# Second-layer expert weights split into half-precision parts inside each job: a perceiver layer on one Trainium2 core

## The reference

```python
def _moe_forward(x, gate_w, gate_b, w1, b1, w2, b2, ln_g, ln_b):
    logits = (x @ gate_w + gate_b) / TEMP
    topk_vals, topk_idx = jax.lax.top_k(logits, TOP_K)
    ...
    h = jnp.einsum('bsd,edf->bsef', x, w1) + b1
    h = jax.nn.gelu(h, approximate=False)
    expert_out = jnp.einsum('bsef,efd->bsed', h, w2) + b2
    out = jnp.einsum('bse,bsed->bsd', gate_probs, expert_out)
    ...
```

## Time and profile before

| | |
|---|---|
| median of three runs | 1473.92 us (1472.44 to 1474.47) |
| the profiled execution's own time | 1473.72 us |
| its span, first to last instruction | 1472.1 us |
| mean granted TensorE clock | 0.972 |
| TensorE busy over the span | 1371.9 us |
| VectorE, ScalarE busy | 780.4 us, 586.5 us |
| groups repeat every | 92.9 us |
| jobs repeat every | 26.4 us |

### The profile page before, as it was taken

How to read it: one execution, slowest core, us unless ns; L and a number is a source line. 1 busy time by engine, 2 the same in 40 slices (tenths; PEclk the granted TensorE clock), 3 DMA queues, 4 the chain that set the end, 5 groups by cost and what they waited for, 6 DMA issues and landing times.

```text
span 1472.1 us, 24339 instructions
## 1 busy us (share of the span) xinstructions
PE 1371.9 (93%) x7888; PEld 870.2 (59%) x7889; DVE 780.4 (53%) x1871; ACT 586.5 (40%) x1082; POOL 152.4 (10%) x200
## 2 busy tenths in 40 slices
PE   6879999999999999999985699999999999999997
PEld 5658677686776876768764344444444444444442
DVE  5665876878778777777665442222222222232225
ACT  3565665756757567465670211212112121121100
POOL 1001012020120200202003100000000000000005
PEclk9999999999999999999996799999999999999997
DMA  9693142341323413224028807523325166100005
GB/s 364 265 351 144 52 156 91 115 160 50 141 95 112 173 50 126 110 97 190 29 114 328 307 17 278 206 93 148 144 104 195 35 265 248 44 21 21 14 15 171
DMA packets 53566, 207.48 MB, mean 141 GB/s; under 512 B 4902, under 2 KB 5012, under 8 KB 47388
## 3 DMA queue, kind: packets, MB, share of 16 engines
q1 hardware_dynamic: 40320, 123.14, 22.8%
q0 software_dynamic: 13184, 83.89, 14.9%
q10 hardware_dynamic: 28, 0.01, 0.0%
HBM read 144.11 MB, written 62.91 MB: 141 GB/s over the span
## 4 chain that ended last, share of the span: by engine, by line
PE 82%; DVE 7%; ACT 4%; issue 4%; DMA 1%; POOL 1%; SPq 0%; DVEq 0%; ACTq 0%
PE bank L623 21%; PE bank L1458 8%; PE bank L1416 7%; PE bank L605 6%; PE bank L606 5%; PE bank L607 5%; PE bank L1379 4%; PE bank L1484 4%; PE bank L1400 3%; PE bank L615 3%; PE bank L1506 2%; PE bank L1425 2%; PE bank L1440 2%; ACT moe_w L951 2%; PE bank L1459 1%
## 5 line engine op out<-in xcount | busy, mean ns | idle before, releaser
L623 PE MATMUL bank<-moe_w,arena 128*128 x736 | 330.9, 592 | 0.0
L491 DVE SCALAR_TENSOR_TENSOR arena<-bank,now_scales,arena 128x512 f32<-128x512 f32 x92 | 69.1, 751 | 346.1 <-PE bank L607 346.1
L623 PEld LDWEIGHTS bank<-moe_w,arena 128*128 128x128 f32 x736 | 132.7, 190 | 132.5 <-issue 132.5
L1416 PE MATMUL bank<-moe_w 128*128 128x257 f32 x768 | 189.9, 385 | 6.5 <-DVE moe_w L883 6.5
L428 ACT ACTIVATE arena<-arena 128x512 f32<-128x512 f32 x92 | 58.3, 633 | 337.8 <-DVE arena L491 337.8
L1416 PEld LDWEIGHTS bank<-moe_w 128*128 128x128 f32 x768 | 138.2, 192 | 25.7 <-DVE moe_w L883 5.8
L605 PE MATMUL bank<-moe_w,arena 128*128 x368 | 140.6, 382 | 2.4 <-DVE arena L504 2.4
L606 PE MATMUL bank<-moe_w,arena 128*128 x368 | 140.4, 382 | 0.0
L607 PE MATMUL bank<-moe_w,arena 128*128 x368 | 140.2, 381 | 0.0
L1458 PE MATMUL bank<-moe_w 128*128 128x512 f16 x384 | 114.4, 379 | 10.0 <-ACT moe_w L940 7.0
L926 ACT ACTIVATE moe_w<-bank,cols,ugain 128x512 f32<-128x512 f32 x96 | 74.6, 777 | 61.6 <-PE bank L1459 60.8
(11 more groups left out here) (230 smaller groups left out, 2129.1 us busy)
## 6 DMA issues: line engine op xcount, KB each, us to landing
moe_w<-w_halves POOLq DMA_DIRECT2D x8, 4096.0 KB, 13.3
moe_w<-in_L_ffn_w_dram POOLq DMA_DIRECT2D x8, 4096.0 KB, 24.4
w_halves<-moe_w SPq DMA_DIRECT2D x48, 512.0 KB, 2.7
xs_rows<-blocks SPq DMA_DIRECT2D x8, 2048.0 KB, 14.8
moe_w<-in_L_ffn_w_dram SPq DMA_DIRECT2D x16, 1024.0 KB, 6.4
arena<-in_ctx_dram SPq DMA_DIRECT2D x32, 384.0 KB
arena<-in_L_ffn_w_dram SPq DMA_DIRECT2D x8, 1024.0 KB, 4.8
blocks<-in_L_ffn_w_dram SPq DMA_DIRECT2D x8, 1024.0 KB, 4.8
```

Of the source, the lines that this page charges most:

```text
L491: nc.vector.scalar_tensor_tensor(out=h_sb[:, fb % 2, :], in0=bank[fb % 2][:, :], scalar=now_scales[:, KD:KD + 1], in1=b1_rows[:, bass.ds(s ...
L623: last = nc.tensor.matmul(Y[:, :], hT_sb[:, fb % 2, c, :], moe_flat[:, bass.ds((e % 2) * 16384 + 8192 + (4 * fb + c) * DIM, DIM)], start=( ...
L1416: last = nc.tensor.matmul(bank[h][:, 0:KEYS], qkT[:, c, b, h * P:(h + 1) * P], cnT[:, b % 2, c, :], start=(c == 0), stop=(c == KC - 1))
```

## The change

The second layer is computed like the first, with three half-precision products instead of a full-precision one. The weights `w2` stay in full precision in memory and in `moe_w`; in each job they are turned into halves, one block's rows (128 x 2048) at a time, in two sets of buffers used in turn (`v_high`, `v_low`, in pieces of 1024 columns): `v_hi` on ScalarE, `v_lo` on VectorE, for block fb once `mm2` of two blocks before is done. The transposed hidden rows are split as well: `h_hi` on ScalarE out of PSUM, `h_lo` on VectorE in place of `hT_copy`. Scales for both are needed: in the first stage `row_sums2` (ScalarE) sums the magnitudes of every w2 row, from loads added to SP (`raw2_load`), and `most_of` and `scales_of` grow. ScalarE's loop in the expert stage becomes a `job` of its own; it holds no load of the activation table any more, only one ahead of it. The second half of the additions to `x_all` is moved from behind job 0 to behind job 1, and `diags` from behind job 1 to behind the last `y_copy`, since v_high and v_low take their space. The diff, cut:

```diff
+        v_high = [[y[:, :], yT[:, :, :].rearrange("p c t -> p (c t)")], [wosT[:, 2, :], wosT[:, 3, :]]]
+        v_low = [[kqT[:, :, :].rearrange("p c t -> p (c t)"), v_sb[:, :]],
+                 [arena[:, 7680:8192], blocks[:, :, :].rearrange("p h t -> p (h t)")[:, 1536:2048]]]
...
+            def h_hi(j, fb):
+                act.wait_ge(hT_full, FB * j + fb + 1)
+                if fb >= 2 or not isinstance(j, int) or j > 0:
+                    act.wait_ge(mm2_done, 1 + FB * j + fb - 1)
+                nc.scalar.activation(hT_high[:, fb % 2, :, :].rearrange("p c t -> p (c t)"), bank[2 + fb % 2][:, :], ACT.Identity,
+                                     scale=now_h[:, 0:1]).then_inc(hT_high_done, 1)
+
+            def v_hi(j, fb, slot):
+                if fb >= 2 or not isinstance(j, int) or j > 0:
+                    act.wait_ge(mm2_done, 1 + FB * j + fb - 1)
+                for i in range(2):
+                    nc.scalar.activation(v_high[fb % 2][i], moe_flat[:, bass.ds(slot * 16384 + 8192 + fb * 2048 + i * 1024, 1024)],
+                                         ACT.Identity, scale=now_v[:, 0:1]).then_inc(v_high_done, 1)
+
+            def job(j, first, last):
+                slot = act.value_load(job_e[0:1, bass.ds(j, 1)], min_val=0, max_val=EXPERTS - 1) % 2
+                gelu(j, 0)
+                if not first:
+                    h_hi(j - 1, 3)
+                act.wait_ge(now_h_ok, j + 1)
+                v_hi(j, 0, slot)
+                gelu(j, 1)
+                h_hi(j, 0)
+                v_hi(j, 1, slot)
+                gelu(j, 2)
+                h_hi(j, 1)
+                v_hi(j, 2, slot)
+                if not last:
+                    x_hi(j + 1)
+                gelu(j, 3)
+                h_hi(j, 2)
+                v_hi(j, 3, slot)
...
+            def h_scales_now(j, e):
+
+                if not isinstance(j, int) or j > 0:
+                    dve.wait_ge(hT_out, FB * j)
+                    dve.wait_ge(v_low_done, 2 * FB * j)
+                nc.vector.tensor_copy(now_v[:, :], job_scales[:, bass.ds(e, 1), KD + 1])
+                nc.vector.tensor_copy(now_h[:, :], job_scales[:, bass.ds(e, 1), KD + 2]).then_inc(now_h_ok, 1)
...
-            def hT_copy(j, fb):
...
+            def h_lo(j, fb):
+                dve.wait_ge(hT_high_done, FB * j + fb + 1)
...
+            def v_lo(j, fb, slot):
+                for i in range(2):
+                    dve.wait_ge(v_high_done, 2 * (FB * j + fb) + i + 1)
+                    nc.vector.scalar_tensor_tensor(out=v_low[fb % 2][i], in0=moe_flat[:, bass.ds(slot * 16384 + 8192 + fb * 2048 + i * 1024, 1024)],
+                                                   scalar=now_v[:, 0:1], in1=v_high[fb % 2][i],
+                                                   op0=ALU.mult, op1=ALU.subtract).then_inc(v_low_done, 1)
...
                 bias(j, 0, slot)
                 if not first:
-                    hT_copy(j - 1, 3)
+                    h_lo(j - 1, 3)
+                h_scales_now(j, e)
+                v_lo(j, 0, slot)
                 bias(j, 1, slot)
-                hT_copy(j, 0)
+                h_lo(j, 0)
                 if not first:
                     y_copy(j - 1)
+                y_scale_now(j, e)
+                v_lo(j, 1, slot)
                 bias(j, 2, slot)
-                hT_copy(j, 1)
+                h_lo(j, 1)
+                v_lo(j, 2, slot)
                 bias(j, 3, slot)
                 if not last:
                     dve.wait_ge(h_biased, FB * (j + 1))
                     scales_now(j + 1)
-                hT_copy(j, 2)
-                if not last:
                     x_lo(j + 1)
+                h_lo(j, 2)
+                v_lo(j, 3, slot)
...
+                pe.wait_ge(v_low_done, 2 * (FB * j + fb + 1))
                 for c in range(4):
...
+                    nc.tensor.matmul(Y[:, :], hT_low[:, fb % 2, c, :], high, start=(fb == 0 and c == 0), stop=False)
+                    nc.tensor.matmul(Y[:, :], hT_high[:, fb % 2, c, :], high, start=False, stop=False)
+                    last = nc.tensor.matmul(Y[:, :], hT_high[:, fb % 2, c, :], low, start=False, stop=(fb == 3 and c == 3))
...
+                if later:
+                    sp.wait_ge(sum2_done, KD * (g - 1) + 3)
+                    raw2_load(g - 1, 3, raw2)
+                    sp.wait_ge(sum2_done, KD * g)
+                    raw_load(g, 0)
...
+                sp.wait_ge(m_full, M_FILLS * g + O_AT + 2)
+                raw2_load(g, 0, raw2)
+                raw2_load(g, 1, raw2)
+                if not nxt:
+                    raw2_load(g, 2, raw2_last)
                 halves_store(g, 0)
-                halves_store(g, 1)
                 if nxt:
                     sp.wait_ge(halves_out[0], 32 * (g + 1))
-                    raw_load(g + 1, 0)
+                    raw2_load(g, 2, raw2)
+                halves_store(g, 1)
...
+            def row_sums2(g, k, of):
+
+                act.wait_ge(raw2_in[k], 16 * (g + 1))
+                if k == 0:
+                    at_least(act, sums2_kept, g)
+                nc.scalar.activation(of[k].bitcast(F16)[:, 0:FF], of[k], ACT.Abs, bias=tiny[:, 0:1], scale=W_SUM,
+                                     accum_out=row_sum2[:, k:k + 1]).then_inc(sum2_done, 1)
```

More of the change, by code:

```diff
@@ L42 @@
 X_MAX = 2.0 ** 10
+H_ROWS = 512.0
 GB = P // TOK
@@ L428, in gelu @@
                 nc.scalar.activation(h_sb[:, fb % 2, :], h_sb[:, fb % 2, :], ACT.Gelu).then_inc(h_act, 1)
-            x_hi(0)
[L431 to L437, removed]
+            def h_hi(j, fb):
[28 more added lines that the diff above has]
+                v_hi(j, 3, slot)
+            x_hi(0)
+            job(0, True, False)
+            with act.Fori(1, JOBS - 1) as j:
+                job(j, False, False)
+            job(JOBS - 1, False, True)
+            h_hi(JOBS - 1, 3)
         def moe_dve(dve):
@@ L543, in moe_dve, with x_and_beta @@
             x_lo(0)
+            def x_and_beta(first, n):
+                for t in range(first, first + n):
+                    last = nc.vector.tensor_tensor(x_all[:, t, :], x_all[:, t, :], lnrow[:, 1, :], ALU.add)
+                return last
             job(0, True)
             dve.wait_ge(rows_in, 48)
-            for t in range(GROUPS):
-                last = nc.vector.tensor_tensor(x_all[:, t, :], x_all[:, t, :], lnrow[:, 1, :], ALU.add)
-            last.then_inc(xb_done, 1)
+            x_and_beta(0, GROUPS // 2)
             job(1, False)
+            x_and_beta(GROUPS // 2, GROUPS // 2).then_inc(xb_done, 1)
+            with dve.Fori(2, JOBS - 1) as j:
+                job(j, False)
+            job(JOBS - 1, False, True)
+            h_lo(JOBS - 1, 3)
+            y_copy(JOBS - 1)
             for t in range(GROUPS):
@@ L621, in mm2 @@
                     pe.wait_ge(ys_out, j)
+                pe.wait_ge(v_low_done, 2 * (FB * j + fb + 1))
                 for c in range(4):
-                    last = nc.tensor.matmul(Y[:, :], hT_sb[:, fb % 2, c, :],
-                                            moe_flat[:, bass.ds((e % 2) * 16384 + 8192 + (4 * fb + c) * DIM, DIM)],
-                                            start=(fb == 0 and c == 0), stop=(fb == 3 and c == 3))
+                    high, low = [part[fb % 2][c // 2][:, (c % 2) * DIM:(c % 2 + 1) * DIM] for part in (v_high, v_low)]
+                    nc.tensor.matmul(Y[:, :], hT_low[:, fb % 2, c, :], high, start=(fb == 0 and c == 0), stop=False)
+                    nc.tensor.matmul(Y[:, :], hT_high[:, fb % 2, c, :], high, start=False, stop=False)
+                    last = nc.tensor.matmul(Y[:, :], hT_high[:, fb % 2, c, :], low, start=False, stop=(fb == 3 and c == 3))
                 last.then_inc(mm2_done, 1)
@@ L1019, in body @@
                     w_hi(g, 3)
+                    row_sums2(g, 0, raw2)
+                    row_sums2(g, 1, raw2)
+                if do_a and not nxt:
+                    row_sums2(g, 2, raw2_last)
+                    row_sums2(g, 3, raw2_last)
+                    act.wait_ge(b1_in, 16)
+                    nc.scalar.activation(b1_raw, b1_raw, ACT.Abs, bias=tiny[0:EXPERTS, 0:1], scale=W_SUM,
+                                         accum_out=b1_sum[:, :]).then_inc(b1_summed, 1)
             act.wait_ge(consts, 7)
@@ L1185, in body @@
                     cn_apply(0, 1)
+                if do_b and do_a:
+                    dve.wait_ge(sum2_done, KD * (g - 1) + 2)
                 for i in range(QK_PAIRS):
```

123 lines of the change are left out of this document (85 added, 38 removed).

## The result

The change took 1516.67 us (median of four runs, 1515.59 to 1518.34), the kernel before 1474.2 us beside it: a ratio of 1.0286, 95% interval 1.0271 to 1.0302. The forecast was 1493 us, 1470 to 1510. The direction was right, but the time lies above the range, at the price of the rival "longer still" (1520). The profiled execution has a span of 1514.0 us, against 1472.1.

The account below looks back on a forecast made before the run. TensorE was taken to bound the kernel before, VectorE's written order the change. 1473.7 + 11.6 (expert stage) + 0.5 (groups) + 3.5 (last group) + 0.5 (scales) + 3.4 (end) = 1493.2 us, range 1470 to 1510.

Parts of the forecast that it names:

- longer still: Rival for the expert stage: 26.8 us a job and a clock fall in each, 1520 us, from 1502 on; chance 0.17.
- TensorE's saving: Second layer: twelve half-precision matmuls at 0.216 us, saving 0.85 us a block, 3.4 us a job, 78 us over 23 jobs.
- The added operations: Expert-stage blocks: h_hi 0.70 and v_hi 1.13 us each on ScalarE, h_lo 0.74 and v_lo 1.28 on VectorE.
- The mechanism: Expert stage: VectorE's in-order queue, waiting for ScalarE, sets the job at 25.95 us against TensorE's 23.0.
- Four idles of some 1.3: Sign to look for: four VectorE idles of some 1.3 us a job before h_lo, put down to ScalarE.
- the walk: VectorE's order through one job, summed start to start; bias to h_lo 2.06 us, three times.
- The length of that chain: VectorE's order through one expert job: 25.95 us, a gain of 0.4 us a job.
- The upper end that I had named: Job chain of 26.8 us if each of twelve new waits costs a sequencer instruction, some 0.07 us more.
- The clock: Expert stage: TensorE's clock falls in six of ten jobs, 1.2 us each, 0.7 us a job, +15.4 us.
- the better case: Rival for the expert stage: VectorE's order bounds but the clock holds, 1478 us, 1475 to 1485; chance 0.2.
- The total: Whole kernel: expert stage +11.6 us, without the clock -3.8; with the terms outside it, 1493.2 us.
- Outside the jobs: First stage and end: groups +0.5 us, last group +3.5, longer chain of scales +0.5, diags at the end +3.4.

Follow-up runs that it names:

- e3: The change with the second layer computed with two products instead of three (low hidden by high weights left out): 1519.18 us, ratio 1.0322.
- e8: The change with h_hi before gelu, diags later, all scales copied at once, and the next job's x_lo ahead of the fourth bias: 1404.79 us, ratio 0.9540.
- e1: The change with only ScalarE's order altered: in each block, h_hi of the block before stands ahead of gelu: 1454.83 us, ratio 0.9873.
- e2: The change with v_lo made for only 16 of 1024 columns per piece from the second job on: 1430.48 us, ratio 0.9708.
- e7: The change with all eight scales of a job copied at once, a job ahead, into two alternating buffers: 1444.51 us, ratio 0.9809.
- e4: The change with 22 unneeded half-precision matmuls added on TensorE behind each job's last second-layer product: 1496.28 us, ratio 1.0162.
- e6: The change with the sixteen diags moved behind the two copies of the transposed probabilities, and their wait behind the bias matmuls: 1510.42 us, ratio 1.0264.
- e9: The change with only the second layer's three scales kept in two alternating buffers, written behind the fourth bias: 1493.02 us, ratio 1.0128.
- e10: The kernel of e9 with 16 unneeded matmuls of 256 columns in TensorE's wait at each job's start: 1465.73 us, ratio 0.9945.

## Why the prediction missed

- **TensorE's saving:** right in size. The twelve matmuls stand 0.216 us apart; e3 and e8 show that the saving counts for nothing in the change and for 3.4 us a job once the order lets it.
- **The added operations:** right. `v_lo` 1.28 us, `v_hi` 1.15 and 1.13, `h_lo` 0.75, `h_hi` 0.68, for 1.28, 1.13, 0.74 and 0.70.
- **The mechanism:** right, shown by e1, e2 and e7. VectorE's order sets the job, with three idles of 1.27 us and one of 0.49 in front of `h_lo`. "Four idles of some 1.3" was a slip in the list of signs: the walk itself had the full distance from bias to `h_lo` only three times, and so it is.
- **The length of that chain: the first term that was mis-sized.** Predicted 25.95 us, measured 26.74 (e4). Bias to `h_lo` is 2.03 for 2.06, a pair of `v_lo` 2.40 as priced. The missing 0.8 lies where small things are handed over: `h_lo` to the first `v_lo` 2.78 for 2.35 (1110.60 to 1113.38; the copies wait 0.25 for VectorE's own write and take two steps, then `v_hi` starts 0.34 behind the second and `v_lo` 1.31 behind that), `h_lo` to the `v_lo` behind `y_copy` 1.79 for 1.5, and `h_lo` to `v_lo` 1.15 for 1.04, twice. The sum of these is 0.94, less 0.15 from the other terms. The upper end that I had named, 26.8, was the right value, but by luck: its reason, a sequencer instruction at each of twelve new waits, would have lengthened bias to `h_lo` too, and that was 2.03 for 2.06. Over the nineteen whole jobs 0.79 x 19 = 15 us.
- **The clock: the second mis-sized term.** "It falls in six of ten jobs", 0.7 us a job. It fell in all 22, at 0.94 us each over the nineteen whole jobs: 0.24 x 19 = 4.6 us more. The price of one fall that I had taken, 1.2, was a little high; the frequency was too low, though both rows of a wait that long had ended in a low stretch. I had weighed the better case against them without a row for it. The Trainium skill, "TensorE: Matmul & The Clock Gate", section "Loop structure matters more than you think", names VectorE's emptying of PSUM as something that leaves the array warm. Here TensorE waited for VectorE itself, and e4 shows that 20 us hung on it.
- **The total:** the expert stage was forecast at +11.6 us and came to +34.0, 22.4 more. The nineteen whole jobs have 19.6 of it, by the two terms above. The first job has 2.4: +2 was a guess without a row, and it took 4.4 more than before. The last job has 0.6, and jobs 1 and 2 cost 5.2 where 5.4 was forecast. The rival "longer still", 26.8 a job with a fall in each, is what happened; it had 0.17. The reason that I gave for it, that one late hand-off returns four times, isn't what the rows show: what came too late comes once a job (0.43 and 0.29 us) or twice (0.11).
- **A slip of sum:** with the clock's 15.4 us at nothing the total is 1477.8, not "below 1477"; nothing rests on it.
- **Outside the jobs:** the key copy at 784.42 (forecast "near 784"), `diags` 3.0 us at the copies and 4.2 at the end (3.4), where e6 gives back 4.6 (I haven't tested where the 1.2 us beyond the 3.0 come from); the start of the expert stage 3.7 us later (4.5). In eleven profiles with the change's first stage it lay between 824.3 and 829.0 us, so this number is good to some 2 us.
- **Why the clock's price is 1.6 us in e9 and 0.94 in the change** can be read from the rows of e9 and e10: a fall hits two places of the circle in e9, 1.00 us at the bias and 0.94 - 0.36 = 0.58 at `v_hi`, which waits until the second layer frees its buffer. In the change `v_hi` waits for the small copy `now_h` at that place instead, which hides the second. I have not isolated this by a run of its own.

## What to carry to other kernels

When work is moved from a full engine to two emptier ones, don't add up their busy time; walk the in-order queue of each and look for an operation that stands directly behind the one it depends on through another engine. Here exchanging `h_hi` and the gelu in ScalarE's order, four times a job, was worth 62 us, some 20 of them the clock's, and three one-number copies of 0.15 us, moved out of it, shortened the circle by 1.4 us a job. If the walk leaves TensorE waiting for over 2 us in each round, as here, price its clock as fallen each time, and shorten that wait first: it costs twice, by itself and by the clock.

## What the runs showed of the hardware

- Waits of TensorE once a job, and the granted clock behind them: 0.4 to 0.6 us, 0.7 to 0.8, 0.9, 1.35 and 1.81 us (e10, e2, e4, e7, e1) left it at 1.00 from the sixth job on; 2.2 to 2.4 us (e9) were followed by slow jobs in most cases, with an undisturbed one every fifth or sixth; 2.6 to 3.0 us (the change) and 4.8 us (e3) were followed by a low stretch every time. The length of the wait alone doesn't decide it. Two of the first, uneven jobs (the third job's start in e6, behind 3.25 us, and in e7, behind 1.97 us) went the other way:

```profile
879.05:883.05 4.00, 4.00 (x21) 2.14 (x22) 3.60 (x4) 2.04 (x2) 0.00 (x0) 1.00 0.00 0
878.75:882.75 4.00, 4.00 (x11) 1.51 (x12) 3.61 (x5) 1.89 (x2) 0.00 (x0) 0.57 0.00 0
```

- The loss doesn't follow the wait's length: 1.6 us a job at 2.2 to 2.4, 0.94 at 2.6 to 3.0, 1.1 at 4.8 (from 910.49 to 1440.01 in e3, 19 jobs, 27.87 each, less 26.74, as VectorE's order is that of the change).
- The jobs of the change aren't alike, though they do the same: 27.35 to 28.6 us in a pattern in which the long one returns after nine jobs (1075.57 to 1104.18, and 1324.72 to 1353.34); in e3 it returns after six. With the clock held (e4) they agree within 0.08 us, so the pattern belongs to the clock.
- ScalarE's `v_hi` takes 1.15 us with and without a full `v_lo` of VectorE beside it on the same weights (e2): no contention between the two was measurable.
